# Recurrence with one matmul per inter-chunk group, a repeated column, and small steps in another order

## The reference

```
q = layernorm(x);  k = v = ctx
ig, fg = gates from concat(q, k, v)                # 8 heads each
cs     = cumsum(log_sigmoid(fg))
log_D  = cs[s] - cs[t] + ig[t]   for t <= s
D      = exp(log_D - max_t log_D)
C      = (q @ k.T / 8) * D
h      = C / (max(|sum C|, exp(-max)) + eps) @ v
x1     = x + headwise_norm(h) * out_w
```

## Time and profile before

| | us |
|---|---|
| median of 3 runs | 1764.92 |
| lowest, highest | 1760.19, 1766.95 |
| the profiled execution's own time | 1758.67 |
| its span, first to last instruction | 1756.9 |

### The profile page before, as it was taken

How to read it: one execution, slowest core, us unless ns; L and a number is a source line. 1 busy time by engine, 2 the same in 40 slices (tenths; PEclk the granted TensorE clock), 3 DMA queues, 4 the chain that set the end, 5 groups by cost and what they waited for, 6 DMA issues and landing times. The chain is left out here.

```text
span 1756.9 us, 58211 instructions
## 1 busy us (share of the span) xinstructions
PE 1550.4 (88%) x21967; PEld 1260.3 (72%) x22095; DVE 1345.8 (77%) x2826; ACT 1153.6 (66%) x2775; POOL 1235.7 (70%) x1235
## 2 busy tenths in 40 slices
PE   4899999999999999999999999769999969898983
PEld 3677777777777777777777777569999945555541
DVE  2578877877887787788778777768777357999998
ACT  3677777777777777777777776513334338888873
POOL 1477677777777767776776777846887528979664
PEclk9899999999999999999999999979999979999998
DMA  6132222223222222322222210174565353777777
GB/s 224 41 105 94 93 92 93 92 97 101 97 93 92 92 92 93 103 99 92 92 92 92 95 66 33 44 278 117 169 202 156 98 120 94 219 216 228 229 217 215
DMA packets 82020, 217.72 MB, mean 124 GB/s; under 512 B 13136, under 2 KB 14544, under 8 KB 72784
## 3 DMA queue, kind: packets, MB, share of 16 engines
q1 hardware_dynamic: 71504, 180.42, 32.9%
q0 software_dynamic: 10240, 33.56, 6.6%
HBM read 146.82 MB, written 67.11 MB: 122 GB/s over the span
## 5 line engine op out<-in xcount | busy, mean ns | idle before, releaser
L315 POOL TENSOR_TENSOR rec_hn<-rec_hn,rec_out_w 128x512 f32<-128x512 f32 x128 | 199.8, 1561 | 180.1 <-DVE rec_hn L741 180.1
L293 POOL TENSOR_TENSOR rec_hrs<-rec_harg,rec_minus_half 128x8 f32<-128x8 f32 x128 | 253.8, 1983 | 10.0
L539 ACT ACTIVATE rec_d<-rec_l_ps 128x512 f32<-128x512 f32 x256 | 150.5, 588 | 41.7 <-PE rec_l_ps L447 41.3
L707 DVE TENSOR_TENSOR rec_c<-rec_s_ps,rec_d 128x512 f32<-128x512 f32 x256 | 164.5, 684 | 17.0 <-PE rec_s_ps L423 16.7
L1005 PE MATMUL exp_q_ps<-exp_wqkv,exp_rows_t 128*128 128x192 f32 x1024 | 177.1, 326 | 0.0
L1336 POOL TENSOR_TENSOR out_x_half<-out_x_half,ln_b 128x512 f32<-128x512 f32 x104 | 132.9, 1284 | 55.9 <-DVE out_z L1512 55.2
L956 POOL DMA_INDIRECT exp_x_rows<-x_scratch,rowid x128 | 135.3, 1057 | 45.6 <-issue 24.2
L761 DVE TENSOR_TENSOR rec_x_ring<-rec_x_ring,rec_hn 128x512 f32<-128x512 f32 x128 | 88.6, 692 | 100.5 <-POOL rec_hn L315 100.0
L1005 PEld LDWEIGHTS exp_q_ps<-exp_wqkv,exp_rows_t 128*128 128x128 f32 x1024 | 165.4, 190 | 0.1
L1065 ACT ACTIVATE exp_rows_t<-exp_t_ps 128x512 f32<-128x512 f32 x128 | 69.4, 594 | 139.6 <-PE exp_t_ps L993 139.6
L467 PE MATMUL rec_o_ps<-rec_v_one,rec_c 128*64 128x65 f32 x4096 | 151.9, 225 | 7.9 <-DVE rec_c L707 7.9
(11 more groups left out here) (217 smaller groups left out, 4370.6 us busy)
## 6 DMA issues: line engine op xcount, KB each, us to landing
rec_x_ring<-in_x SPq DMA_DIRECT2D x128, 256.0 KB, 2.8
rec_ctx_ring<-in_ctx SPq DMA_DIRECT2D x128, 256.0 KB, 3.0
x_scratch<-rec_x_ring SPq DMA_DIRECT2D x128, 256.0 KB, 2.0
out_x_half<-x_scratch SPq DMA_DIRECT2D x104, 256.0 KB, 4.9
out<-out_x_half SPq DMA_DIRECT2D x104, 256.0 KB, 5.6
exp_wqkv<-in_wqkv SPq DMA_DIRECT2D x4, 1536.0 KB, 7.9
v_all<-x_scratch SPq DMA_DIRECT2D x24, 256.0 KB, 5.1
out<-v_all SPq DMA_DIRECT2D x24, 256.0 KB, 5.6
```

The source lines that it names most:

```text
L293: nc.gpsimd.tensor_tensor(hrs[:, G % 2], harg[:, G % 2], mhalf[:], ALU.pow).then_inc(hrs_done, 1)
L315: nc.gpsimd.tensor_tensor(h, h, w8[:], ALU.mult).then_inc(hw_done, 1)
L539: nc.scalar.activation(dst[:].rearrange("p k s -> p (k s)"), l_ps[:], ACT.Exp).then_inc(l_read, 1)
L707: vec.tensor_tensor(cmat[e][:].rearrange("p k s -> p (k s)"), s_ps[e][:], dmat[e][:].rearrange("p k s -> p (k s)"), ALU.mult).then_inc(c_d ...
```

## The change

- `log_inter` has one matmul for each of the four head pairs, where there were two. Partitions 64 to 127 of `rows` now hold, for chunks 1 to 3, the last column of the chunk before, repeated 128 times, and `sel_q` holds the selection on partitions 0 to 63 and its negative on 64 to 127.
- VectorE makes that repeated half with a second copy (64 x 384) in the `rows` stage, before it raises the semaphore.
- The first scores of a batch, `scores(g+1)` in step 3, stand behind the `rows` stage and `turn_hat`, ahead of `log_decay`; step 0 has none at its start.
- `turn_x1` stands between the two `log_decay` of step 3, and ahead of the `logits` transpose in step 0.
- ScalarE copies the finished chunk (`put_x1`) before the exponent of the second decay matrix, not behind it, in every step; in step 3 it copies the normalised input before the first exponent.
- `cumsum` stands behind `products` on the matmul engine; VectorE reads `gates` and `cumsum` after `peaks`, `head_norm` and `inter_queries`.

```diff
-    sel_q = sb("sel_q", [P, 2, KC, P], BF16)
+    sel_q = sb("sel_q", [P, KC, P], BF16)
...
-                nc.tensor.matmul(o, sel_q[:, 0, k, :], src[:, c * P:(c + 1) * P], start=(k == 0), stop=False)
-                mm = nc.tensor.matmul(o, sel_q[:, 1, k, :], src[:, c * P - 1:c * P].broadcast_to([P, P]),
-                                      start=False, stop=(k == KC - 1))
+                mm = nc.tensor.matmul(o, sel_q[:, k, :], src[:, c * P:(c + 1) * P], start=(k == 0), stop=(k == KC - 1))
...
         for g in steps:
-            last = g % 4 == 3
-            if valid(g):
+            last, early = g % 4 == 3, g % 2 == 0
+            if valid(g) and g % 4:
                 scores(g)
...
-            if order.gate_key(g, 0) and not last:
+            if order.gate_key(g, 0) and early:
                 gate_group(order.gate_key(g, 0))
             if valid(g):
                 products(g)
-            if order.gate_key(g, 0) and last:
+            if order.gate_key(g, 0) and not early:
                 gate_group(order.gate_key(g, 0))
             if valid(g + 8) and last:
                 turn_hat(g + 8)
+            if valid(g + 1) and last:
+                scores(g + 1)
             if valid(g + 1):
                 log_decay(g + 1, 0)
+            if valid(g - 3) and last:
+                turn_x1(g - 3)
...
             if valid(g + 1):
                 log_decay(g + 1, 1)
+            if valid(g - 3) and not last:
+                turn_x1(g - 3)
             if order.gate_key(g, 2):
                 gate_group(order.gate_key(g, 2))
-            if valid(g - 3):
-                turn_x1(g - 3)
...
+            if valid(g + 8) and g % 4 == 3:
+                put_hat(g + 8)
             if valid(g + 1):
                 decay_matrix(g + 1, 0)
-            if valid(g + 8):
+            if valid(g + 8) and g % 4 < 3:
                 put_hat(g + 8)
...
+            if valid(g - 3):
+                put_x1(g - 3)
             if valid(g + 1):
                 decay_matrix(g + 1, 1)
-            if valid(g - 3):
-                put_x1(g - 3)
...
-            vec.tensor_copy(sel_q[:, 0, :, o], m4[:, e, :, o])
-            vec.tensor_scalar(sel_q[:, 1, :, o], m4[:, e, :, o], -1.0, None, ALU.mult)
+            vec.tensor_copy(sel_q[0:64, :, o], m4[0:64, e, :, o])
+            vec.tensor_scalar(sel_q[64:P, :, o], m4[0:64, e, :, o], -1.0, None, ALU.mult)
...
             elif kind == "rows":
-                vec.tensor_copy(rows[p][0:64, :], sm_ps[0:64, 0:256].bitcast(BF16)).then_inc(sm_read, 1)
+                read = sm_ps[0:64, 0:256].bitcast(BF16)
+                vec.tensor_copy(rows[p][0:64, :], read)
+                vec.tensor_copy(rows[p][64:P, P:].rearrange("p (c s) -> p c s", c=NC - 1),
+                                read[:, P - 1:S - 1:P].unsqueeze(2).broadcast_to([64, NC - 1, P])).then_inc(sm_read, 1)
...
-            if order.gate_key(g, 0) and g % 4 < 3:
+            if order.gate_key(g, 0) and g % 4 == 2:
                 gate_step(order.gate_key(g, 0))
...
+            if order.gate_key(g, 0) and g % 4 < 2:
+                gate_step(order.gate_key(g, 0))
             if valid(g - 1):
                 variances(g - 1)
```

## The result

| | before | after |
|---|---|---|
| median, us | 1763.50 (6 runs) | 1750.43 (6 runs) |
| lowest, highest | 1760.19, 1766.95 | 1745.15, 1757.55 |
| the profiled execution's own time | 1758.67 | 1757.55 |
| ratio of after to before | | 0.9932 (0.9910 to 0.9953) |

The change makes the kernel 0.7% faster, 13 us. The forecast was 1705 us (60 us), with 1684 to 1738 as its range: the sign was right, the size was wrong by more than a factor of four.

The account below looks back on a forecast made before the run. The prediction took the matmul engine, 92% busy, as the bound. Its terms summed to 1.87 us a batch, 59.8 over 32 batches, taking 1758.67 to 1698.9; adding 6.25 for the runs' median gave 1705 us, range 1684 to 1738.

Parts of the forecast that it names:

- the sum: All terms together on the matmul engine: 1.87 us a batch gained, 59.8 us over 32 batches.
- the 0.5 that the prediction had named as a sign of being wrong: Products waiting for VectorE's multiplies (L707) by more than 0.5 us a batch would show the forecast wrong.
- VectorE is the bound: Rival: VectorE's busy time and waits come to 34.2 us a batch against 34.29; 1762 us, no change; chance 0.08.
- VectorE's need: Argument against VectorE as the bound: without the two gate waits (2.76 us) it needs 31.4 us a batch.
- Matmuls: Inter-chunk factor: 384 matmuls removed at 56 ns each, 21.5 us in all, 0.67 us a batch gained.
- nothing on the matmul engine: Second copy for `rows`: 0.41 us on VectorE (0.31 to 0.68), covered for the matmul engine by the scores' 1.16 us.
- ScalarE's exchange and the logits: Copying the finished chunk before the exponent gains 0.95 us a batch at the context's transpose; later logits gain 0.21.
- First scores: Scores moved behind the rows cover a 0.19 us wait, against a new 0.15 in step 0: net 0.04 a batch.
- Gates and cumulative sum: Later cumulative sum and VectorE gate reads: counted as 0 for the matmul engine, bounds -0.3 to +0.3 us a batch.
- No cost below is one of a slow clock: Premise: the clock stands at its higher level, 2.4 GHz, almost throughout the recurrence.
- The slower rival: Rival: ScalarE's exchange ends each second decay matrix's exponent 0.48 us late; 1805 us, or 1774 at every second chunk; chance 0.05.
- only the matmuls, 1743: Rival: only the removed matmuls' 21.5 us is gained, as idle time returns one instruction later; 1743 us, chance 0.14.

Follow-up runs that it names:

- e10: The changed kernel with GpSimd's step-1 sum of the forget gates' logs moved behind the weighing of the keys; 1713.2 us, 0.9719 of the kernel before.
- f1: The kernel before with only GpSimd's sum of the logs moved behind the weighing of the keys; 1751.3 us, 0.9919 of the kernel before.
- e2: The kernel before with only the four-matmul inter-chunk factor and its repeated column, in the old order; 1772.2 us, 1.0065 of the kernel before.
- f6: e10 with the inter-chunk factor back in eight matmuls and one copy for `rows`; 1726.2 us, 0.9782 of the kernel before.
- f4: e10 with the finished chunk's transpose and copy, and step 3's copy of the normalised input, at their old places; 1738.7 us.
- f3: e10 with the first scores of a batch back at the start of step 0; 1729.6 us, 0.9792 of the kernel before.
- e3: The changed kernel with the cumulative sum and VectorE's reads of gates and cumulative sum at their old places; 1758.9 us, 0.9986 of the kernel before.
- e6: The changed kernel with the finished chunk's transpose and copy, and step 3's copy of the normalised input, at their old places; 1753.6 us.
- e1: The changed kernel with the first scores of a batch back at the start of step 0; 1742.5 us, 0.9898 of the kernel before.
- e8: The changed kernel with VectorE's product of the m ends replaced by four small matmuls and the first scores back at the start of step 0; 1734.6 us.
- e9: The changed kernel with VectorE's offsets of step 1 moved right behind the two multiplies; 1744.6 us, 0.9899 of the kernel before.
- e5: e2 with the decay matrices reading only partitions 0 to 63 of `rows` and waiting for the first copy alone; 1768.3 us.

## Why the prediction was wrong, point by point

*What bounds the kernel: the step that failed.* "So the matmul engine sets the pace, and what counts is its instructions and the short waits between them." From this the sum let every matmul and wait that went shorten the batch in full, 1.87 us, and gave the reordering on VectorE nothing, "since that engine hardly waits for VectorE here". The runs show another path level with the matmul engine: ScalarE's logarithm, GpSimd's logs, keys, values and product (L300, L267, L278, L315), VectorE's residual, scan and statistics, then the multiplies that the products of step 2 need. As the matmul engine got faster the products' wait rose from 0.23 to 1.12 us a batch, 0.9 of the 1.26 that the sum was too high, past the 0.5 that the prediction had named as a sign of being wrong. e10 cuts one link of the path, takes no work away, and gains 1.00 us a batch; f1 gains 0.46 with the same step in the kernel before.

*Why the rival did not warn me.* "VectorE is the bound" had the right engine, and even named the chains through GpSimd and ScalarE, but it priced them at 1762, no change. It added VectorE's busy time and its waits and compared the sum with a batch. These two add up to nearly the whole time by themselves (633.8 and 158.8 us of the 800 before the change), so the sum could not tell a bound from an engine that idles. Nor did VectorE's need fall to 31.4 with the gate waits gone: it was busy 687.5 us in 800 against 633.8, with the second copy at 0.55 us and the queries' multiply, three a batch, at a mean of 1.20 in place of 0.68.

*Matmuls, 0.67 us a batch.* 56 ns each was right. Alone they lose (e2); with everything in their favour the net is 0.30 (f6 against e10). The second copy took 0.55 us, inside the bounds, but "nothing on the matmul engine" holds only with the scores in front: in e2 the wait for `rows` rose to 0.69.

*ScalarE's exchange and the logits, 1.16.* The waits fell as forecast (25.7 to 7.0, 7.4 to none), and the context's new wait of step 0 is there as a wait of 0.16 one group later (L434). The worth was 0.38, and the products' wait is 0.5 longer with this part than without it. Without the chain it is 0.92 (f4), near the sum.

*First scores, 0.04.* 0.00 in the changed kernel, 0.43 with the chain gone (f3).

*Gates and cumulative sum, 0 (bounds -0.3 to +0.3).* 0.53 (e3): outside the bounds, and the largest of the three parts that were taken back one at a time in the changed kernel. The three (0.53, 0.38, 0.00) don't add up to the 0.61 of the whole.

*The clock* was no term. "No cost below is one of a slow clock" was true of the kernel before. At the products' wait of 1.1 us ten falls came, of 1.3 us each, more than half of what the batches gained.

*The slower rival* (ScalarE's exchange hurts) did not come: e6 is slower by 0.38 us a batch, not faster.

*The range.* It took every term at full size together. The least case, "only the matmuls, 1743", was not a least: e2 shows that they alone can cost 0.65%, 11 us. That the measured 1750 lies in that rival's band (1735 to 1755) is chance: the waits did not come back as it says, the matmuls alone did not gain, and the clock, in neither account, took 13 us in the profiled execution.

## What to carry to other kernels

A matmul engine at 92% with small waits can share the pace with a path over the other engines. Before pricing its waits, follow one late operand of the next batch back over the engines, instruction by instruction; where it passes an engine whose queue begins with a wait, the order there can be worth more than matmuls removed. Here one line moved on GpSimd gave 0.8% before the change and 2.1% after it (the clock falls that went are part of the latter). And where a path holds, parts are not additive: the scores and the finished chunk were worth 0.00 and 0.38 us a batch with the path in place, and 0.43 and 0.92 without it. Adding up an engine's busy time and waits does not say whether it is the bound.

## What the hardware did that was not expected

- The clock fell to 1.2 GHz for 3.4 us at a wait of only 1.05 to 1.19 us between matmuls, ten times in one execution, and in e3 at one of 0.70 us; never at 0.9 us in e1, and never at the 1.08 us for `rows` in e8. One fall costs 1.3 us. The length of the wait alone does not decide it, and why the same wait brings a fall in one batch and not in the next stays open.
- VectorE's multiply of the state's queries (L718), two inputs in SBUF, took 0.68 us where no GpSimd instruction was running as it began, and 1.37 to 1.53 where GpSimd's keys (L267) were, ending about 0.55 us behind them; its mean over 800 us went from 0.68 to 1.20 only because it now starts at another moment. Where L718 began first, GpSimd's product (L315) took 1.66 us in place of 1.27. The Trainium skill's "SBUF — State Buffer", section "Who interferes with whom", has this rule (two SBUF inputs on VectorE against a read of GpSimd, and the order of issue decides who is blocked), and the trace agrees with it. What a hold costs in time is another matter: e9 took one of 1.0 us away and gained 0.08 us a batch, since a later wait took up the rest.
- Copying 384 bf16 columns of a column repeated 128 times took 0.55 us, longer than 512 columns that lie side by side (0.41).
- A matmul over 64 partitions started 0.31 us behind one of 512 columns over 128 partitions (e5); with 128 partitions in both it was 0.22 us (e2).
